# Softmax division behind the value product, and nine transfers into two sets of key and query stacks

## What is computed

```
tgt1  = layer_norm(x, g1, be1)
q, k, v = tgt1 @ Wq.T + bq, tgt1 @ Wk.T + bk, tgt1 @ Wv.T + bv      # 16 heads of 16
score = einsum('bshd,bthd->bhst', q, k) / 4 + (1 - mask) * -1e9
p     = softmax(score, axis=-1)
o     = einsum('bhst,bthd->bshd', p, v)
x     = x + (o @ Wo.T + bo) + (ctx @ Wg.T + bg)
out   = x + relu(layer_norm(x, g2, be2) @ W1.T + b1) @ W2.T + b2
```

## Time and profile before

| | |
|---|---|
| median of 3 runs | 1937.09 us (1935.44 to 1938.04) |
| the profiled execution, its span | 1935.5 us, 1933.7 us |
| busy PE, PEld, DVE | 1808.0, 1700.1, 1804.6 us |
| busy ACT, POOL | 1448.5, 1139.6 us |
| transfers | 234.25 MB in 164172 packets, the main queue's packets 46.6% of 16 engines' span |
| granted TensorE clock, mean | 0.993 |

### The profile page before, as it was taken

How to read it: one execution, slowest core, us unless ns; L and a number is a source line. 1 busy time by engine, 2 the same in 40 slices (tenths; PEclk the granted TensorE clock), 3 DMA queues, 4 the chain that set the end, 5 groups by cost and what they waited for, 6 DMA issues and landing times.

```text
span 1933.7 us, 56738 instructions
## 1 busy us (share of the span) xinstructions
PE 1808.0 (93%) x17716; PEld 1700.1 (88%) x17716; DVE 1804.6 (93%) x8535; ACT 1448.5 (75%) x5513; POOL 1139.6 (59%) x1607
## 2 busy tenths in 40 slices
PE   5899999999999999999999999999999999999997
PEld 5789889889889899898898898898898898898987
DVE  6899999999999999999999999999999999999994
ACT  4778778778778778777787787787787787777872
POOL 3556656565566566566566566565665665665663
PEclk8899999999999999999999999999999999999999
DMA  6454454454544544544544534545535545445440
GB/s 173 121 144 105 120 130 114 128 130 109 133 122 114 136 123 109 140 114 115 143 111 116 146 100 125 138 105 129 137 101 134 126 111 135 119 113 140 109 106 23
DMA packets 164172, 234.25 MB, mean 121 GB/s; under 512 B 29984, under 2 KB 114336, under 8 KB 163872
## 3 DMA queue, kind: packets, MB, share of 16 engines
q1 hardware_dynamic: 163872, 230.62, 46.6%
HBM read 62.73 MB, written 16.78 MB: 41 GB/s over the span
## 4 chain that ended last, share of the span: by engine, by line
DVE 54%; issue 21%; ACT 18%; PE 5%; POOL 1%; SPq 0%; DMA 0%; DVEq 0%; ACTq 0%; POOLq 0%
ACT scores L349 13%; DVE scores L586 11%; DVE k_hi L650 6%; DVE stats L486 5%; DVE rstd L514 4%; ACT hid L382 3%; DVE var L494 3%; DVE xhat L523 3%; DVE q_lo L639 3%; DVE hT_hi L625 3%; DVE y L573 2%; DVE sum_inv L529 2%; DVE resid L560 2%; DVE newton L512 2%; DVE mv L491 2%
## 5 line engine op out<-in xcount | busy, mean ns | idle before, releaser
L712 POOL TENSOR_TENSOR scores<-scores,sum_inv 128x512 f32<-128x512 f32 x512 | 549.3, 1078 | 646.5 <-DVE sum_inv L529 646.5
L349 ACT ACTIVATE scores<-scores,row_min 128x128 f32<-128x128 f32 x2048 | 796.4, 397 | 174.5 <-DVE row_min L586 169.6
L586 DVE CUSTOM_DVE_ANT_0 scores<-score_ps,mask_bias 128x128 f32<-128x128 f32 x2048 | 470.9, 285 | 1.0 <-issue 1.0
L359 ACT ACTIVATE probs<-turn_ps 128x512 f32<-128x512 f32 x512 | 301.8, 590 | 191.9 <-PE turn_ps L829 191.9
L349 ACT ACTIVATION_READ_ACCUMULATOR scores<-scores,row_min 128x1 f32 x2048 | 400.0, 195 | 0.0
L829 PE MATMUL turn_ps<-ident,scores 128*128 128x128 f32 x2048 | 312.5, 275 | 21.6 <-POOL scores L712 21.4
L768 PE MATMUL ffn_ps<-w_hi,hT_lo 128*128 128x256 f32 x1024 | 304.0, 297 | 26.5 <-DVE hT_lo L630 24.6
L768 PE MATMUL ffn_ps<-zT_hi,w_lo 128*128 128x256 f32 x1024 | 302.7, 296 | 5.0 <-ACT hid L382 3.7
L718 POOL TENSOR_TENSOR hT_lo<-hid,hT_hi 128x512 fp32r<-128x512 f32 x192 | 258.4, 1346 | 69.3 <-DVE hT_hi L625 69.3
L770 PE MATMUL ffn_ps<-zT_hi,w_hi 128*128 128x256 f32 x1024 | 286.8, 280 | 0.0
L769 PE MATMUL ffn_ps<-zT_lo,w_hi 128*128 128x256 f32 x1024 | 286.7, 280 | 0.0
(11 more groups left out here) (115 smaller groups left out, 4623.7 us busy)
## 6 DMA issues: line engine op xcount, KB each, us to landing
k_stack<-k_hi SPq DMA_DIRECT2D x512, 128.0 KB, 2.8
q_stack<-q_hi SPq DMA_DIRECT2D x512, 64.0 KB, 2.0
k_stack<-k_lo SPq DMA_DIRECT2D x256, 128.0 KB, 2.8
x_in<-x_dram SPq DMA_DIRECT2D x64, 256.0 KB, 3.3
mem_in<-memory_dram SPq DMA_DIRECT2D x64, 256.0 KB, 3.6
x_res<-x_dram SPq DMA_DIRECT2D x64, 256.0 KB, 3.0
q_stack<-q_lo SPq DMA_DIRECT2D x256, 64.0 KB, 2.0
out_dram<-y SPq DMA_DIRECT2D x64, 256.0 KB, 2.9
```

The source lines that it names most:

```text
L349: last = act.activation(scores[:, k, h, :], scores[:, k, h, :], ACT.Exp, bias=row_min[:, k, h:h + 1], scale=-1.0, accum_out=row_sum[:, k, ...
L359: act.activation(probs[:, k % CPB, :], turn_ps[k % 2][:, :], ACT.Copy).then_inc(probs_copied, 1)
L586: last = dve.tensor_tensor_reduce(out=scores[:, t, h, :], in0=score_ps[t % 2][:, h * S:(h + 1) * S], in1=mask_bias[:, b, :], scale=1.0, sc ...
L712: pool.tensor_tensor(scores[:, k], scores[:, k], sum_inv[:, k, :].unsqueeze(2).broadcast_to([P, CH, S]), ALU.mult).then_inc(probs_normed, 1)
```

## The change

- GpSimd no longer multiplies the exponentials by the inverse sums. TensorE transposes the undivided exponentials as soon as they are there. VectorE inverts 16 sums at a time (t = 5 and 9), GpSimd spreads each over the 16 features of its head (`spread_inverses`), TensorE transposes the result once a pass (`turn_inverses`, four transpositions more), ScalarE copies it to SBUF (`copy_inverses`, t = 1), and VectorE multiplies the value product by it on its way out of PSUM (`attn`). The high part of `attn` is now taken by ScalarE at t = 4, the low part by VectorE at t = 4.
- The columns of Wq and Wk are reordered at the start (`set_columns`), so that even heads lie in partitions 0 to 63 and odd heads in 64 to 127, and the four partitions that go to one row of the stacks lie together. `k_stack` is zeroed once, in whole, by GpSimd; six transfers of keys then write only the places of the data, 16 partitions each, and three of queries fill `q_stack`. There are two sets of both stacks, used in turn. ScalarE writes `k_hi` directly, and `k_full` and its two multiplications are gone.
- Both 1/sqrt are two GpSimd instructions, an addition and a power (`ALU.pow`).
- The split of `mem_in` (the context) and the last low part of the hidden layer move from VectorE to GpSimd; `x_res` and `resid_b2` are made at other ticks (6 for 4, 0 for 2).

The core of the diff (tiles, semaphores and the setup are left out where they only rename):

```diff
-NEWTON_STEPS = 3
...
-INVERT_TICKS = (1, 2, 3, 5, 5, 7, 7, 9)
-NORM_TICKS = (1, 2, 3, 5, 6, 7, 8, 9)
+INVERT_TICKS = (5, 9)
...
-        k_full = sb("k_full", [P, KT * GB, S])
-        kk = [sb("k_hi", [P, KT * GB, 2, S], F32R), sb("k_lo", [P, KT * GB, 2, S], F32R)]
-        q_stack = sb("q_stack", [P, CPB, KT, ROWS], F32R)
-        k_stack = sb("k_stack", [P, CPB, KT * GB, 2, S], F32R)
+        kk = [sb("k_hi", [P, KT, ROWS], F32R), sb("k_lo", [P, KT, ROWS], F32R)]
+        q_stack = [sb(f"q_stack{n}", [P, CPB, KT, ROWS], F32R) for n in range(2)]
+        k_stack = [sb(f"k_stack{n}", [P, CPB, KT * GB, 2, S], F32R) for n in range(2)]
...
-                    sp.wait_ge(q_split, i + 2)
-                    for r in range(CPB):
-                        if later(i + 1):
-                            sp.wait_ge(scores_ready, CHUNKS * i + CPB + r + 1)
-                        for j, high_low in enumerate((1, 0, 0)):
-                            sp.dma_start(q_stack[32 * j:32 * j + 32, r].bitcast(F32),
-                                         q[high_low][32 * r:32 * r + 32].bitcast(F32)
-                                         ).then_inc(q_stacked, 16)
+                    g = i + 1
+                    if g < 2:
+                        sp.wait_ge(zeros_set, 4)
+                    else:
+                        sp.wait_ge(scores_ready, CHUNKS * (g - 1))
+                    sp.wait_ge(q_split, g + 1)
+                    for j, high_low in enumerate((1, 0, 0)):
+                        sp.dma_start(q_stack[g % 2][32 * j:32 * j + 32].bitcast(F32),
+                                     q[high_low][:].bitcast(F32)).then_inc(q_stacked, 16)
+                    sp.wait_ge(k_split, g + 1)
+                    for e in range(2):
+                        for j, high_low in enumerate((0, 1, 0)):
+                            to = 32 * j + HD * e
+                            sp.dma_start(k_stack[g % 2][to:to + HD, :, :, e, :]
+                                         .rearrange("p r k s -> p (r k) s").bitcast(F32),
+                                         kk[high_low][HALF * e:HALF * (e + 1)]
+                                         .rearrange("p k (b s) -> p (k b) s", b=GB).bitcast(F32)
+                                         ).then_inc(k_stacked, 16)
...
+            def copy_inverses(g):
+                act.wait_ge(inv_turned, g + 1)
+                if later(g):
+                    act.wait_ge(attn_ready, g)
+                act.activation(inv[:].rearrange("p k r -> p (k r)"), turn_ps[0][:, :], ACT.Copy
+                               ).then_inc(inv_copied, 1)
             def iteration(i, norm, front, attn_, out_, ffn):
                 for t in range(TICKS):
                     if out_ and t == 0:
                         copy_turned(i - 1, CHUNKS - 1)
+                    if out_ and t == 1:
+                        copy_inverses(i - 1)
+                    if out_ and t == 4:
+                        g = i - 1
+                        split_high(attn[:], attnT[0], attn_ready, g + 1, proj_ready,
+                                   g if later(g) else None, attnT_hi)
...
+                            act.wait_ge(k_stacked, 16 * 2 * TERMS * g)
                         for k in range(KT):
-                            last = act.activation(
-                                k_full[:, GB * k:GB * (k + 1), :].rearrange("p b s -> p (b s)"),
-                                by_tile[0][:, k, :], ACT.Identity, bias=bkc[:, k:k + 1])
-                        last.then_inc(k_copied, 1)
+                            last = act.activation(kk[0][:, k, :], by_tile[0][:, k, :], ACT.Identity,
+                                                  bias=bkc[:, k:k + 1])
+                        last.then_inc(k_high, 1)
...
-            def invert_sums(i, k):
-                dve.wait_ge(exps_ready, CHUNKS * i + k + 1)
-                dve.reciprocal(sum_inv[:, k, :], row_sum[:, k, :]).then_inc(sums_inverted, 1)
+            def invert_sums(i, b):
+                dve.wait_ge(exps_ready, CHUNKS * i + CPB * (b + 1))
+                if later(i):
+                    dve.wait_ge(inv_spread, GB * (i - 1) + b + 1)
+                dve.reciprocal(sum_inv[:, b], row_sum[:, CPB * b:CPB * (b + 1), :]
+                               .rearrange("p c (k e) -> p k c e", k=KT)).then_inc(sums_inverted, 1)
...
+                        dve.wait_ge(inv_copied, g + 1)
                         if later(g):
-                            dve.wait_ge(proj_ready, g)
-                        dve.tensor_copy(attnT[0][:], value_tiles).then_inc(attnT_hi, 1)
-                        split_low(value_tiles, attnT, attnT_hi, g + 1, attnT_split)
+                            dve.wait_ge(attnT_split, g)
+                        dve.tensor_tensor(attn[:], value_tiles, inv[:], ALU.mult).then_inc(attn_ready, 1)
...
+                    if out_ and t == 4:
+                        split_low(attn[:], attnT, attnT_hi, i, attnT_split)
...
-                        dve.wait_ge(k_copied, g + 1)
-                        if later(g):
-                            dve.wait_ge(scores_ready, CHUNKS * i + CPB)
-                        for e in range(2):
-                            last = dve.tensor_scalar(kk[0][:, :, e, :], k_full[:], par[:, e:e + 1], None,
-                                                     ALU.mult)
-                        last.then_inc(k_high, 1)
                         dve.wait_ge(k_high, g + 1)
-                        for e in range(2):
+                        for k in range(KT):
                             last = dve.scalar_tensor_tensor(
-                                out=kk[1][:, :, e, :], in0=k_full[:], scalar=par[:, e:e + 1],
-                                in1=kk[0][:, :, e, :], op0=ALU.mult, op1=ALU.subtract)
+                                out=kk[1][:, k, :], in0=by_tile[0][:, k, :], scalar=bkc[:, k:k + 1],
+                                in1=kk[0][:, k, :], op0=ALU.add, op1=ALU.subtract)
                         last.then_inc(k_split, 1)
...
+            for n in range(2):
+                pool.memset(q_stack[n][96:P].rearrange("p r k n -> p (r k n)").bitcast(F32), 0.0
+                            ).then_inc(zeros_set, 1)
+                pool.wait_ge(zeros_set, 2 * n + 1)
+                pool.memset(k_stack[n][:].rearrange("p r k e s -> p (r k e s)").bitcast(F32), 0.0
+                            ).then_inc(zeros_set, 1)
+                pool.wait_ge(zeros_set, 2 * n + 2)
...
+            def inverse_root(g, mv, var, rstd, mean_done, var_done, ready, done):
+                pool.wait_ge(mean_done, g + 1)
+                if later(g):
+                    pool.wait_ge(ready, g)
+                pool.tensor_tensor(var[:], mv[:, :, 1], eps[:], ALU.add).then_inc(var_done, 1)
+                pool.wait_ge(var_done, g + 1)
+                pool.tensor_tensor(rstd[:], var[:], minus_half[:], ALU.pow).then_inc(done, 1)
...
+            def spread_inverses(g, b):
+                pool.wait_ge(sums_inverted, GB * g + b + 1)
+                if later(g):
+                    pool.wait_ge(inv_turned, g)
+                pool.tensor_tensor(inv_rows[:, b].rearrange("p k (h d) -> p (k h) d", d=HD),
+                                   sum_inv[:, b].rearrange("p k c e -> p (k c e)").unsqueeze(2)
+                                   .broadcast_to([P, H, HD]),
+                                   one[:, :].unsqueeze(2).broadcast_to([P, H, HD]), ALU.mult
+                                   ).then_inc(inv_spread, 1)
...
-                    if attn_ and t in NORM_TICKS:
-                        k = NORM_TICKS.index(t)
-                        pool.wait_ge(sums_inverted, CHUNKS * i + k + 1)
-                        pool.tensor_tensor(scores[:, k], scores[:, k],
-                                           sum_inv[:, k, :].unsqueeze(2).broadcast_to([P, CH, S]),
-                                           ALU.mult).then_inc(probs_normed, 1)
-                    if ffn and t in HIDDEN_TICKS[:HJ - 1]:
+                    if ffn and t in HIDDEN_TICKS:
                         g, n = i - 2, HIDDEN_TICKS.index(t)
-                        pool.wait_ge(hid_hi, HJ * g + n + 1)
-                        pool.tensor_tensor(hT[1][:, 2 * n:2 * n + 2, :], hid[:, n % 2],
-                                           hT[0][:, 2 * n:2 * n + 2, :], ALU.subtract
-                                           ).then_inc(hid_split, 1)
+                        if n == 0 and later(g):
+                            pool.wait_ge(down_ready, g)
+                        split_low(hid[:, n % 2], [h[:, 2 * n:2 * n + 2, :] for h in hT], hid_hi,
+                                  HJ * g + n + 1, hid_split)
+                    if attn_ and t == 6:
+                        spread_inverses(i, 0)
+                    if attn_ and t == 10:
+                        spread_inverses(i, 1)
+                    if out_ and t == 2:
+                        g = i - 1
+                        pool.wait_ge(mem_loaded, 16 * (g + 1))
```

(37 more changed lines are left out.)

162 lines of the change are left out of this document (60 added, 102 removed).

## The result

The changed kernel takes 1939.9 us (median of 20 runs, 1937.93 to 1942.52), the kernel before 1937.07 (20 runs, 1935.44 to 1939.44). The ratio is 1.0016, with a 95% interval of 1.0009 to 1.0023: slower by 3 us, where 1909 was forecast. The profiled execution took 1938.98 us, with a span of 1937.4. In later runs the kernel before took either about 1937 us or about 1950, both of them on two of four chips, while the changed kernel kept to one level (1937.9 to 1942.5 us over 37 runs), so new kernels are set against the changed kernel.

What follows compares the result with a forecast made beforehand. VectorE was taken to bound the kernel, TensorE following; afterwards ScalarE's run plus TensorE's path. A pass falls from 29.29 to 28.92 us: 1935.5 - 23 (61 passes) - 5 (start and end) = 1907.5, median 1909 us; range 1850 to 1970.

Steps and rivals of the forecast that it cites:

- What bounds the kernel, and the waits set free: VectorE leads and TensorE follows; TensorE's waits on VectorE and GpSimd, 2.49 us a pass at most, can go.
- The tie to ScalarE's run: Projection waits for attnT_hi at the end of ScalarE's run: 12.61 us from x turn, TensorE idle 1.76 us.
- The first rival: ScalarE's run doesn't bind, so TensorE sets the pass at 27.16 us: 1800 us in all; chance 0.10.
- The term from projection to x turn: TensorE's path in a pass, 18.20 us, becomes 16.31 without its waits and with four new transpositions.
- Four transpositions take 0.36 us to the next start: Spacing on TensorE's timeline, used to price the four added transpositions at + 0.36 us a pass.
- Start and end ... I take - 5: Passes that fill and drain against extra stack fills and column reordering: - 5 us, bounds - 12 to + 6.
- The keys: Six key transfers, at half rate 7.3 us, ready at 13.4 us behind projection's start, wanted at 15.1: hidden.
- the rival on the other side: Keys late: lateness past 15.1 us after projection's start lengthens every pass; up to 2210 us; chance 0.12.
- The power: GpSimd's power in each norm takes 0.3 us, hidden; the rival, over 1.4 us each, had chance 0.08.
- the cover of 1.4 us: Time each GpSimd power ahead of the next pass's xhat may take and still stay hidden.
- VectorE held up in its first half: Rival: VectorE loses its 1.2 us of slack before attnT_lo; 29.3 us a pass, 1930 us; chance 0.18.

Runs made afterwards that it cites:

- s1: r2 with the stacks of keys laid out with the parities apart, so key transfers write pieces of 2 KB instead of 512 bytes; 1840.78 us.
- e1: Changed kernel, but VectorE makes attnT_hi itself at t = 2, behind the product with the inverses, instead of ScalarE at t = 4; 1865.45 us.
- e2: Changed kernel, but ScalarE makes attnT_hi ahead of the exponentials of the fourth chunk instead of behind them; 1863.9 us.
- e3: Changed kernel, but the four transpositions of the inverses are made twice, to the same places; 1967.08 us.
- r3: r2, but the second set of stacks is filled only behind the second norm's root, and TensorE doesn't wait for fills; 1905.64 us.
- r2: e1, but VectorE also makes the low part attnT_lo at once at t = 2 instead of at t = 4; 1908.71 us.
- s3: s1 and r3 together: longer key pieces and the late second fill; 1838.23 us.
- s2: Changed kernel with only the stacks of keys laid out as in s1, in pieces of 2 KB; 1933.82 us.
- u1: The kernel before, unaltered, run again on one chip; 1937.14 us once and 1950.1 to 1950.3 us three times.
- u2: The changed kernel, unaltered, on the same chip as u1; 1940.22 us.
- r4: Changed kernel with six more key transfers a pass, to the otherwise zero halves of the stacks, all twelve waited for; 2472.16 us, single run.

## Why the prediction was wrong

**What bounds the kernel, and the waits set free: right.** All five waits of the earlier trace rows went; with nothing in the way (s1) a pass is 27.55 us, where I had 27.16. VectorE fell to 19.3 us a pass (19 forecast), GpSimd to 13.1 (12), ScalarE rose by 0.7 (1.1).

**The tie to ScalarE's run: right in mechanism and size.** X turn to projection takes 12.54 us (1027.03 to 1039.57 above), I had 12.61; the wait is 1.91 - 0.36 = 1.55 us, I had 1.76. e1 and e2 show the cause from two sides. The first rival, that the run doesn't bind, is refuted.

**The term from projection to x turn was too small**: 16.31 predicted, 16.61 measured (602.46 to 619.07, and the median of all passes). The step that failed is "Four transpositions take 0.36 us to the next start": it was taken from a place where a product follows. Ahead of other transpositions it is 0.44, and e3's four more cost 0.42. That counts at three places of the path, 0.24 of the 0.30. With it, the pass is 29.14 instead of 28.92: 0.22 x 61 = 13.4 us of the miss.

**"Start and end ... I take - 5" was the larger miss**: + 12.7 us (10.05 and 2.6), even outside the bounds of - 12 to + 6. I had credited the passes that fill and drain with waits on VectorE that would go, and charged too little for what is new there. The step that failed is this - 5, a sum in which the lighter VectorE outweighs the fills, and in which the first transfers have no price.

- The first x turn comes 3.0 us later (14.64 against 11.68), and the first queries with it. Most of that is the second set's fill, which stands ahead of the norm's root and holds VectorE's copies and conversions of weights while it lasts: in r3 the x turn is back at 12.04. Taken out of the way, together with TensorE's wait for it, it gives back 2.6 to 3.1 us of the whole time (r3 against r2, s3 against s1). This part is shown.
- From the first queries to the first scores it takes 5.3 us more. This was in no term. Before, the first scores waited for the queries and only the first three of the twelve transfers of keys, issued at 28.50, and began 3.7 us later; the changed kernel has one semaphore for all six, issued from 26.28 on, and begins at 40.55. The transfers of the first group are hidden by nothing. The longer pieces give back 1.74 us of this (s2); waiting for a part of the keys wasn't tried, so the rest is argued from the timelines.
- 1.7 us more are lost by the x turn of pass 3, and 2.6 at the end. Their cause stays open. In both kernels TensorE runs part of the first 110 us at the lower clock (mean granted clock of 20 to 110 us: 0.85 before and 0.83 after, 0.83 and 0.79 in u1 and u2), and what that costs wasn't separated.

13.4 and 17.7 (- 5 to + 12.7) make 31.1 us: from 1907.5 to 1938.6, against 1938.98 profiled.

**The keys: right that they were hidden, 2.7 us ahead of need where I had 1.7, and partly by luck.** Six transfers of keys were costed at 7.3 us, and the three of queries, 786 KB in front of them in the same queue, at nothing. The queries move at 129 GB/s, so they take 6 us, and all nine 15 to 16. In the changed kernel that did little harm, because the first keys are issued only at 1013.45, when the queries issued from 1007.70 on have nearly moved (the rate falls from 125 to 73 GB/s at 1014); the keys were there by 1023 and wanted at 1025.69. Once `attnT_hi` is VectorE's, the keys are issued 4.5 (e1) and 3.9 us (r2) behind the queries instead of 5.75, and stand behind them. e1 brings TensorE to the projection 1.3 us sooner and just has no wait; r2 takes 0.3 more and starts the queries 0.9 later, and waits. So the rival on the other side was the next wall behind the one I described, not a remote one. By the Trainium skill, SBUF — State Buffer, "Door 1: The DMA port swizzle", where the rate goes by the ports reached, 16 partitions would give about 109 GB/s and the queries' 32 about 218; the trace has 97 and 120 with 16 partitions, by the length of the pieces, and 129 with 32. The measurement decides: here the pieces' length mattered, and the page's ratio of two didn't show.

**The power: mis-sized, without effect.** 0.69 to 0.71 us instead of 0.3, between the two rows I had taken as bounds and under the cover of 1.4 us.

**VectorE held up in its first half: not in the changed kernel, but in e1 and r2.** In the changed kernel VectorE waits 1.20 us for `attnT_hi`, and `attnT_lo` takes its usual 0.69. The Trainium skill, SBUF — State Buffer, "Who interferes with whom", says that VectorE's copies and conversions in a two-port mode contend with GpSimd, that an operation with two inputs in SBUF contends with a GpSimd instruction that reads SBUF, and that one then waits for the other's whole instruction. The traces agree: 3.69 us beside a fill of 3.54, 1.23 for 0.42 beside `memT_hi`, 1.66 for 0.69 beside `memT_lo`.

## What to carry to other kernels

When work is taken off the engine that sets the pace, look at where in its new queue each moved instruction stands: `attnT_hi` in front of the fourth chunk's exponentials instead of behind them is worth 76 us (e2). Count all transfers ahead of the one that is waited for, and the length of the pieces that each writes: a buffer's order of dimensions was worth 6 us by itself and 68 once TensorE was free. A transfer that is hidden in the steady state is waited for in the first pass; sum the start from its own timeline.

## What was not expected of the hardware

- Transfers from SBUF to 16 partitions moved at 97 GB/s in pieces of 512 bytes (DMA share 1.28) and at 120 in pieces of 2 KB (1.07); to 32 partitions, out of 128 partitions at the source, at 129 GB/s (1010 to 1013 in the changed kernel), while 32 out of 32, in pieces of 4 KB, had given 215. Whether the source's spread or the pieces make that last difference wasn't tried.
- In r4's wait of 6.1 us TensorE's granted clock fell from 1.00 to 0.50 and stayed there until 1017; in the waits of 1.3 and 1.4 us shown above, of the changed kernel and r2, it stayed at 1.00.
- Four transpositions cost 0.44 us in front of a transposition and 0.36 in front of a product.
- A fill by GpSimd held VectorE's conversion for its whole length (3.69 us for 0.43) and itself took 3.54 us in place of 3.52. In the changed kernel the second set's fills took 2.04 and 3.75 us for 1.80 and 3.52, beside VectorE's scaling of Wq, 3.56 for 0.61. Nearly all of the cost fell on VectorE.
